# Second phase: ScalarE instead of VectorE takes the router's result out of PSUM

## The reference

```python
# x: (32, 128, 56, 56)
x = x + conv_ref(ln_c(x), ...)       # sign, 3x3 conv with binarised weights, batch norm, relu
t = to_tokens(x)                     # (32, 3136, 128)
u = ln_t(t)                          # layer norm over the 128 channels
weights = u @ wr + br                # the router: one number per token
idx = top_k(weights, 1568)[:1567]    # the chosen tokens of the image
h = gelu(u @ w1 + b1)                # 128 -> 512
y = h @ w2 + b2                      # 512 -> 128
x = t + u + where(chosen, y * weights, 0)
```

## Time and profile before

| | |
|---|---|
| Median of 3 runs | 2020.09 us (2017.94 to 2023.11) |
| Profiled execution | 2015.51 us, its span 2013.7 us |
| PE busy | 1852.1 us, 92% of the span |
| DVE busy | 1568.3 us, 78% |
| ACT busy | 1214.9 us, 60% |
| POOL busy | 1143.0 us, 57% |
| Mean granted TensorE clock | 0.977 |

### The profile page before, as it was taken

The page is one execution under the profiler, slowest core; times in us unless marked ns, Lnnn a source line. Parts: engine busy times, 40 slices in busy tenths (PEclk is TensorE's granted clock), DMA queues, the critical chain, the costliest instruction groups (busy, mean ns, idle before and its releaser), DMA issues.

```text
span 2013.7 us, 32702 instructions
## 1 busy us (share of the span) xinstructions
PE 1852.1 (92%) x8507; PEld 992.6 (49%) x8507; DVE 1568.3 (78%) x4488; ACT 1214.9 (60%) x2030; POOL 1143.0 (57%) x907
## 2 busy tenths in 40 slices
PE   7789989759999999999999999999999999999996
PEld 4557666634444444444444444444444444444443
DVE  3487677867888788888888888888888888888875
ACT  5466666446666566666666666666666666666653
POOL 3465666364655556556565556665666555555543
PEclk8899999969999999999999999999999999999998
DMA  5677888511333333333333333333333333333213
GB/s 221 246 280 289 295 331 304 199 40 65 129 119 127 110 125 118 118 118 118 122 123 122 125 119 117 119 134 116 119 117 119 125 122 117 120 127 124 99 71 133
DMA packets 82074, 294.08 MB, mean 146 GB/s; under 512 B 23920, under 2 KB 28864, under 8 KB 81984
## 3 DMA queue, kind: packets, MB, share of 16 engines
q1 hardware_dynamic: 68880, 242.40, 33.0%
q10 hardware_dynamic: 13104, 50.72, 6.7%
HBM read 213.80 MB, written 78.07 MB: 145 GB/s over the span
## 4 chain that ended last, share of the span: by engine, by line
PE 51%; DMA 10%; DVE 6%; SPq 6%; issue 3%; POOL 1%; ACT 1%; ACTq 0%; DVEq 0%; POOLq 0%
PE ps L1168 25%; PE ps L1157 6%; PE ps L1158 5%; PE ps L1159 5%; PE ps L1113 5%; SPq L504 4%; DMA wse<-w_row 4%; DMA w_row<-wrow 3%; PE ps L1146 2%; DMA y16a<-y_int 2%; DMA y16b<-y_int 2%; SPq L510 1%; DVE base L910 1%; POOL rm L592 1%; ACT hs L670 1%
## 5 line engine op out<-in xcount | busy, mean ns | idle before, releaser
L1168 PE MATMUL ps<-hs,w_c 128*128 128x448 f32 x1792 | 765.9, 555 | 0.4 <-ACT yo L680 0.4
L670 ACT ACTIVATE hs<-ps,b1c,undo 128x448 f32<-128x448 f32 x896 | 609.8, 719 | 128.6 <-PE ps L1159 121.7
L578 POOL TENSOR_TENSOR tl<-tr,th 128x448 f16<-128x448 f32 x224 | 243.7, 1089 | 306.1 <-PE ps L1159 187.7
L1168 PEld LDWEIGHTS ps<-hs,w_c 128*128 128x128 f32 x1792 | 313.9, 191 | 209.3 <-issue 177.6
L573 POOL TENSOR_TENSOR xb<-xb,zr 128x448 f32<-128x448 f32 x224 | 261.4, 1169 | 265.6 <-ACT zr L697 264.9
L1157 PE MATMUL ps<-th,w_h 128*128 128x448 f16 x896 | 318.4, 355 | 17.0 <-ACT hs L670 17.0
L585 POOL TENSOR_TENSOR yo<-yo,base 128x448 f32<-128x448 f32 x221 | 277.1, 1260 | 75.6 <-DVE yo L987 75.6
L1159 PE MATMUL ps<-th,w_l 128*128 128x448 f16 x896 | 316.1, 353 | 0.0
L1158 PE MATMUL ps<-tl,w_h 128*128 128x448 f16 x896 | 316.1, 353 | 0.0
L680 ACT ACTIVATE yo<-ps,cols 128x448 f32<-128x448 f32 x224 | 141.7, 633 | 240.0 <-PE ps L1168 239.8
L1074 PE MATMUL ps<-packs,cwT 128*128 128x448 f32 x1008 | 245.9, 397 | 1.7 <-DVE y16a L759 1.7
(11 more groups left out here) (146 smaller groups left out, 2376.5 us busy)
## 6 DMA issues: line engine op xcount, KB each, us to landing
xb<-x SPq DMA_DIRECT2D x48, 896.0 KB, 4.6
xb<-x SPq DMA_DIRECT2D x48, 672.0 KB, 4.4
result<-yo SPq DMA_DIRECT2D x32, 896.0 KB, 3.5
gate_all<-gate_row ACTq DMA_DIRECT2D x31, 896.0 KB, 4.4
result<-yo SPq DMA_DIRECT2D x32, 672.0 KB, 3.0
gate_all<-gate_row ACTq DMA_DIRECT2D x31, 672.0 KB, 5.5
base<-x SPq DMA_DIRECT2D x16, 896.0 KB, 10.1
hs<-mean_row SPq DMA_DIRECT2D x14, 896.0 KB, 5.1
```

The source lines that it names most:

```text
L578: nc.gpsimd.tensor_tensor(cut(tl, c), tr[(b + c) % 2][:, :], cut(th, c), ALU.subtract).then_inc(tl_ready, 1)
L670: nc.scalar.activation(hs[(b + slot) % 2][:, j, :], ps[:, H_BANK + j, 0:T], ACT.Gelu_apprx_tanh, bias=b1c[:, j:j + 1], scale=undo[:, 1:2]) ...
L1168: last = M(bank, w2_c[:, j, :], hs[(b + c) % 2][:, j, :], start=first, stop=final)
```

## The change

The step that takes the router's result out of PSUM moves from DVE's list to ACT's. On DVE it stood alone at position 27, before the base of a token chunk. On ACT it stands at position 27 behind the GELU of that position and before everything else due there. The operation is the same, `wrow = ps * undo + br`; ACT does it as an `Identity` activation with `scale` and `bias`. The semaphores are the same. For the last image the position is 21, where ACT has no GELU.

```diff
@@ scalar engine, phase2, behind the GELU and the taking of y @@
+                    for m, mb, _ in due(ROUTER_AT.later(1), 0, n, b, pos):
+                        act.wait_ge(w_done, m + 1)
+                        if has(m - 1):
+                            act.wait_ge(w_saved, m * 32)
+                        nc.scalar.activation(wrow[:, :], ps[:, T_BANK, 0:T], ACT.Identity, bias=br_c,
+                                             scale=undo[:, 0:1]).then_inc(w_taken, 1)
@@ vector engine @@
-            def take_router(n):
-                dve.wait_ge(w_done, n + 1)
-                if has(n - 1):
-                    dve.wait_ge(w_saved, n * 32)
-                V.tensor_scalar(wrow[:, :], ps[:, T_BANK, 0:T], undo[:, 0:1], br_c,
-                                ALU.mult, ALU.add).then_inc(w_taken, 1)
...
-                    for m, mb, _ in due(ROUTER_AT.later(1), 0, *at):
-                        take_router(m)
```

## The result

The changed kernel takes 2130.69 us, the median of four runs (2124.4 to 2131.92); the kernel before, in the four runs beside it, 2019.01 (2015.58 to 2023.11). The ratio is 1.0546, 95% interval 1.0517 to 1.0575: slower by 111.7 us. Predicted were 2122 us, 2080 to 2152. The profiled execution took 2131.92 us, its span is 2129.8 us against 2013.7.

A forecast was written before the change was run, and what follows sets the result against it. PE was taken as the bound, interrupted once per image by the router's path through DRAM. The profiled 2015.5 us + 72 delay + 30 clock gave 2117.5; with the median 4.6 us above that execution, 2122 us, range 2080 to 2152.

The forecast's parts named there:

- The bound: Second phase: PE is the bound, interrupted once per image by the router's DRAM path, without slack between L510 and PE.
- DVE's relief priced at nothing: DVE without L917: some 1.7 us back per image, priced at nothing because DVE's later waits only grow.
- ACT's work priced at nothing: The added Identity on ACT: 633 ns, 757 at the other end, costing nothing because ACT has room.
- the wait of 4.74 us: ACT's idle time before its second `zr`, waiting for the load of `y16b`; cited as room for the Identity.
- The delay: Router result to PE's count: L510 2.32 us later in 31 images, 72 us, bounds 54 and 76.
- The clock: Granted clock falling behind PE's longer waits: 40 us less 10 for the GELU wait, so 30 us.
- the 3.66 us wait: PE's wait at 147.74 in the earlier trace: clock 0.63 over the next 8 us, 3.0 us lost.
- three in four: Share of PE's 3.7 us waits taken to lower the clock, at 1.7 us each: 40 us.
- The delay alone: Rival 1: clock stays at 2.4 GHz behind PE's longer waits; 2092 us, 2074 with the short path; chance 0.25.
- The faster case: Rival 3: DVE bounds the count and its relief shortens PE's waits; 2000 us, at most down to 1979; chance 0.03.
- the case in which SP's queue hides more: Rival 2: L510 only 0.5 to 1.2 us late, 16 to 37 us, 2036 to 2057; chance 0.07.
- The signs: Profile marks: Identity about 0.63 us, L510 within 0.1 us of its end, PE's count wait 3.4 to 3.9 us.

The follow-up runs named there:

- e6: Kernel before, DVE taking the router's result at position 30 behind four additions without use: 2158.76 us against 2023.22, ratio 1.0662.
- e7: Kernel before, DVE taking the router's result at position 30 behind three additions without use: 2131.74 us against 2018.41, ratio 1.058.
- v1_split: Kernel before, with the second of the two w_row DMAs issued by ACT's queue ahead of the GELU: 1997.33 us against 2019.76, ratio 0.9879.
- e1: Kernel before, with DVE taking the router's result at position 30 instead of 27: 2020.2 us against 2019.76, ratio 1.000.
- e4: Changed kernel plus 16 unused matmuls on PE ahead of each image's first count, except the last image: 2089.18 us against the kernel before's 2019.76, ratio 1.0358.
- e3: Changed kernel, with ACT taking the router's result at position 25 ahead of that position's GELU: 2050.37 us against the kernel before's 2019.76, ratio 1.0137.
- v4_split_count37: Kernel before with ACT issuing the second w_row DMA and the first count at 37 instead of 36: 2002.6 us against 2023.22, ratio 0.9898.

## Why the prediction was right

*The bound.* PE with one interruption per image, of which every link from L510 on is waited for: shown from both sides. A later L510 costs whoever causes it (e6, e7), and a shorter link gains (v1_split: 0.70 us earlier, 22 us less, and 31 x 0.70 = 22).

*DVE's relief priced at nothing.* Right: what it got back is in two longer waits of DVE, and e1 shows the same without the change.

*ACT's work priced at nothing.* Right, by the pair of e7 and the changed kernel, to within their intervals of some 0.7%. The reading behind it was incomplete: between its place and the wait of 4.74 us ACT does not one GELU but three, and `th` besides. The room was there even so: in the image shown of the changed kernel ACT still waits 1.12 us for DVE before its `th` at 1049.78. I sized it wrongly: the nearest row I chose was L680 with 0.633 us, and it took 0.73 us, near the other end, L697's 0.757, which also reads both scale and bias from SBUF.

*The delay.* I predicted L510 2.32 us late; it was 2.49 in the image shown. The Identity was 0.10 us longer, SP reacted 0.19 us after its end and not 0.03 as in the last image, and the start came 0.09 us earlier than I had it. From L510 to the count it was 6.21 us instead of 6.33, so of the 0.57 us that an emptier queue could have given, 0.12 came (0.05 by the medians over the images, 6.21 and 6.26). The term was 72 us; by the waits it is 75.6, and e4, which removes the clock, leaves 70.

*The clock.* The mechanism was right, the term too small: 30 us, where e4 measures 41. I took three waits in four at 1.7 us each, 40 us, less 10 for the GELU. The clock was low behind 30 of 31 waits, ten of them with a loss like that of the 3.66 us wait. Between the first and the last router PE was busy 52.3 us longer, and 15.3 came back in the wait for the GELU, so 37.0 net.

The "three in four" rested on a wrong count. I wrote that the kernel before has nine waits of 1.87 us and more in all; these were the ones between the convolutions and the one of the second phase. There are six more in the first phase, of 2.36, 3.33, 6.04, 8.51, 9.38 and, at the start, 9.75 us. Without the one at the start, every wait of over 3 us in that trace has a low stretch behind it, six of six: 3.66 and 8.98 us, with 0.63 and 0.75, and these four (stretch, length, busy PE with its instructions, clock, DMA share, GB/s; the last two lie in one stretch that reads 0.50 throughout):

```profile
18.30:26.30 8.00, 6.76 (x16) 0.50 0.81 335
404.20:412.20 8.00, 6.65 (x28) 0.66 0.00 2
419.90:427.90 8.00, 1.25 (x5) 0.50 0.03 5
426.50:434.50 8.00, 4.78 (x11) 0.50 0.00 0
```

The three of my nine without one were of 2.28, 2.55 and 2.93 us. So for waits of 3.7 us the trace already said nearly every one, and my 0.75 mixed them with shorter ones. What I cited from the Trainium skill, "TensorE: Matmul & The Clock Gate", section "HAM oscillation — how this bites in real kernels", was the better guide to how often: the clock falls at nearly every such wait. The sum by it, 2145 us, was further from the measured 2130.69 than mine, 14 us against 9, since it took nothing off for the wait for the GELU. With waits of 1.9 us the clock fell at 11 of 31 (e3), so the "every" holds for these long ones and not in general.

*The rivals.* The delay alone would have been 2092 us; e4 is that kernel, with 2089. The faster case and the case in which SP's queue hides more are out: L510 was the full 2.49 us late. The sum of 102 us was short by 10, nearly all of it the clock's term.

*The signs.* Three of those I named did not hold as given: the Identity took 0.73 us and not about 0.63, L510 came 0.19 us behind its end and not within 0.1, and PE's wait lay outside the 3.4 to 3.9 us that I gave in four of the 31 images (from 3.1 to 4.1 us).

## What to carry to other kernels

Before a step is moved to another engine because that engine has time, read what stands ahead of it in that engine's list, DMA issues among it, and who waits for its result. ACT was busy 60% and DVE 78%, and yet the step was worse off on ACT, since its result starts a chain of small DMAs that PE waits for. Look at such a chain before the engines' busy shares: here it paid to split its issues over two queues (v1_split, 22 us), and to put what starts it ahead of the GELUs in its list (e3, 81 us). And price a longer wait of PE higher than its length; here 70 us of delay brought 41 us of low clock with them.

## What the runs showed that I had not expected

- An engine's slack can swallow an experiment: moving the taking on DVE by three positions moved it by 0.08 us.
- Giving PE and DVE the first count one position later did not take PE's wait for it away but made it longer, 0.87 us instead of 0.54 (v4_split_count37).
- Of the linked additions of 128x448 on DVE the second took 1.44 us and the others 0.61 to 0.62, with 0.03 us between one and the next. POOL's addition L587 runs beside the first two and ends 0.48 us before the second does. In the first image, where POOL has no such addition there, all four took 0.62. So the link costs little. That POOL's addition holds the second one up is what these rows suggest; no run here took it away. The image shown with POOL, and the first one:

```profile
1046.49 2.52 POOL L587 TENSOR_TENSOR yo<-yo,base 128x448 f32<-128x448 f32 x1 [1.23 <-DVE yo L993]
1047.41 3.40 DVE L921 TENSOR_TENSOR idle<-kt 128x448 f32<-128x448 f32 x4
...
462.64 2.60 DVE L921 TENSOR_TENSOR idle<-kt 128x448 f32<-128x448 f32 x4 [0.92 <-PE ps L1130]
```
